# Attention and a mixture of experts on one core: score products in two row halves over three banks, a second norm one step later, fewer small vector operations

## The chip, the cores and the metric

One core of one Trainium2 chip. The metric is the device time of one execution, in microseconds. The programs are written directly against the engines: TensorE (PE), VectorE (DVE), ScalarE (ACT), GpSimd (POOL) and SyncE (SP) each have their own list of instructions, and semaphores hold them together.

## What is computed

`x` and `ctx` are 32 batches of 64 tokens with 128 features, float32. First comes cross attention with 16 heads of 8 features, then a mixture of 16 experts with two chosen per token plus one shared expert, each on a layer norm and each added to `x`:

```python
qh, kh, vh = heads(layernorm(x) @ Wq.T), heads(ctx @ Wk.T), heads(ctx @ Wv.T)
scores = einsum('bhqd,bhkd->bhqk', qh, kh) / scale          # scale = 8 ** -0.5
scores = where(mask, -1e9, scores)
x = x + merge(softmax(scores) @ vh) @ Wo.T
flat = layernorm(x)
top, idx = top_k(flat @ router_w.T + router_bias, 2)
combine = scatter(softmax(top), idx)                         # tokens x 16 experts
out = sum_k combine[:, k] * ((silu(flat @ gate_k) * (flat @ up_k)) @ down_k)
x = x + out + (silu(flat @ sh_gate.T) * (flat @ sh_up.T)) @ sh_down.T
```

## The kernel before, in words

The 2048 tokens are 16 tiles of 128 rows, two batches each. Everything that feeds a float32 product of the experts is split into a high and a low part (`w_hi`, `w_lo`, `xt2_hi`, `xt2_lo`, `hid_hi`, `hid_lo`), so that three fast products stand for one exact one.

**Projections.** Four groups of four tiles: first norm on DVE (`norm1`, `scale1`, L634 to L651), transposes, masks, and the products for V, Q and K on TensorE (`project`, L872). Q and K land in `q_all` and `k_all` with the features of eight heads in 64 rows for one batch and 64 for the other, and two halves of the heads one behind the other.

**Attention, the pipeline of 16 steps.** Each engine has a function `step(t, p, on)`; `on(lag)` says whether tile `t - lag` exists. In step `t`:

- POOL masks Q and K of tile `t + 2` into `q_blk` and `k_blk` (`q_block`, `k_blocks`, L414 to L430), and finishes the second norm's factors of tile `t - 2`.
- PE (L936 to L1003) makes the two score products of tile `t + 1` (128 rows, 512 columns each, `scores(g)`, L964), transposes the two halves of the probabilities of tile `t` (`transposes(h)`, L945), multiplies them with V (`values(h)`, L954), turns the value sums of tile `t - 1` back into rows (`values_as_rows`, L914), transposes its attention row (`attention_transposed`, L919) and projects it (`output_projection`, L924), and for tile `t - 2` transposes the second norm (`norm_transposed`, L930) and makes the router product (`router`, L934).
- DVE (L700 to L771) adds the projection to `x` (L705), adds the router's bias (L708), takes the moments of the second norm (L713, L721) and the two best experts (L717 to L733), takes the row maxima of the scores (L738), subtracts them (L759), and divides the value sums (L747, L749).
- ACT (L532 to L574) copies the transposed probabilities (L542), scales the second norm (L554), copies the transposed attention row (L558) and the transposed second norm twice (L564, L565), takes the exponentials (L547), copies the value sums (L570), and casts a piece of the expert weights (L538).

**What sets the order.** The order of calls in these functions, written out by hand, engine by engine; each engine works through its list in order. PSUM has eight banks; two of them hold scores (`score_ps`), so that the first score product of the next tile may be written once DVE has subtracted that of this one.

**Experts.** Four groups of 512 tokens, nine units each (the shared expert and eight pairs): `gate`, `up`, `down` on PE (L1028 to L1073), SiLU and the high part on ACT (`silu`, `high_part`), product, low part and weight on DVE (`product`, `low_part`, `weighted`). The first units run between the last steps of the attention; this stretch, from step 15 to the first dense units, is called the hand-over below. Outside the pipeline's loop the last steps are called by `peel(step, TILES)` and so on.

## Time and profile before

| | |
|---|---|
| median of 3 runs | 193.76 us (193.52 to 194.12) |
| the profiled execution | 194.68 us, span 192.9 us |
| PE busy | 179.3 us (93% of the span) |
| DVE busy | 168.8 us (87%) |
| ACT busy | 124.6 us (65%) |
| POOL busy | 92.1 us (48%) |
| chain that ended last | PE 61%, DVE 19%, ACT 5%, issue 5% |

The span is what the profile sees of the profiled execution; the rest of its time lies around it. An engine's busy time is the union of its instructions. A product on TensorE in float32 appears as two records, a transpose as one; their ends are modelled, so it is the distance from one start to the next that tells what one costs. The stages: projections to about 34 us, attention to about 103, the hand-over to about 124, experts to the end.

### The profile page before, as it was taken

How to read it: one execution, taken by the hardware profiler on the slowest of the kernel's cores; microseconds unless marked ns; L12 is line 12 of the kernel's file. 1: busy time of each engine (PE TensorE's matmuls, PEld its weight loads, DVE VectorE, ACT ScalarE, POOL GpSimd, SP SyncE). 2: the span in 40 equal slices, each digit the busy share in tenths (PEclk: the TensorE clock that was granted, in tenths of full speed). 3: DMA queues.
4: the chain of work that ended last, by engine and by line, in shares of the span. 5: the costliest groups of instructions: out<-in, count | busy, mean ns of one | idle time of the engine just before them, and what ended most of it. 6: DMA issues, size and time to landing. Idle time of an engine off the chain costs nothing.

```text
span 192.9 us, 4173 instructions
## 1 busy us (share of the span) xinstructions
PE 179.3 (93%) x1351; PEld 131.8 (68%) x1351; DVE 168.8 (87%) x515; ACT 124.6 (65%) x280; POOL 92.1 (48%) x148
## 2 busy tenths in 40 slices
PE   7599599999999999999998799999999999999962
PEld 7497467566666666666666466778888888888841
DVE  6899999589999999989995799988899889988981
ACT  2168374777888888888885855466655665565641
POOL 5746992758988988888786690300000000000000
PEclk9969979999999999999999999999999999999997
DMA  5984910000000000000000174332363236324401
GB/s 135 286 249 92 352 40 0 5 0 0 3 2 5 0 3 0 3 0 2 5 0 3 57 198 139 110 110 82 128 180 115 72 126 171 120 82 126 120 0 54
DMA packets 13202, 15.33 MB, mean 79 GB/s; under 512 B 1665, under 2 KB 8193, under 8 KB 13057
## 3 DMA queue, kind: packets, MB, share of 16 engines
q1 hardware_dynamic: 12608, 14.57, 24.8%
q10 hardware_dynamic: 576, 0.55, 1.2%
q8 instruction: 9, 0.15, 0.3%
q14 instruction: 9, 0.07, 0.1%
HBM read 13.93 MB, written 1.18 MB: 78 GB/s over the span
## 4 chain that ended last, share of the span: by engine, by line
PE 61%; DVE 19%; ACT 5%; issue 5%; POOL 0%; DVEq 0%; POOLq 0%
PE bank L1013 26%; PE bank L964 12%; PE bank L945 5%; PE bank L954 5%; DVE hid L823 2%; PE bank L903 2%; ACT hid_hi L598 2%; PE bank L934 2%; DVE prob L759 2%; PE bank L924 2%; DVE smax L738 2%; DVE xn L649 2%; DVE hid_lo L815 2%; DVE cmix_sb L823 2%; PE bank L893 1%
## 5 line engine op out<-in xcount | busy, mean ns | idle before, releaser
L589 ACT ACTIVATE sig<-bank 128x512 f32<-128x512 f32 x36 | 21.5, 600 | 21.0 <-PE bank L1013 20.4
L964 PE MATMUL bank<-k_blk,q_blk 128*128 128x512 f32 x64 | 34.0, 615 | 0.0
L426 POOL TENSOR_TENSOR k_blk<-k_all,consts_sb 128x512 f32<-128x512 f32 x32 | 32.7, 1045 | 0.0
L1013 PE MATMUL bank<-xt_hi,w_hi 128*128 (+1 forms) x72 | 29.1, 405 | 0.0
L1013 PE MATMUL bank<-xt_lo,w_hi 128*128 (+1 forms) x72 | 28.4, 394 | 0.0
L1013 PE MATMUL bank<-xt_hi,w_lo 128*128 (+1 forms) x72 | 28.3, 393 | 0.0
L542 ACT COPY prob_t<-bank 128x512 f32<-128x512 f32 x32 | 18.8, 586 | 11.5 <-PE bank L945 11.5
L806 DVE TENSOR_TENSOR hid_u<-sig,bank 128x512 f32<-128x512 f32 x32 | 21.9, 684 | 4.2 <-PE bank L1013 2.5
L738 DVE TENSOR_REDUCE smax<-bank 128x8 f32<-128x512 f32 x32 | 21.9, 686 | 2.6 <-PE bank L964 2.6
L759 DVE TENSOR_TENSOR prob<-bank,smax 128x512 f32<-128x512 f32 x32 | 22.0, 687 | 0.6
L547 ACT ACTIVATE prob<-prob 128x512 f32<-128x512 f32 x32 | 20.8, 653 | 0.0
L945 PE MATMUL bank<-consts_sb,prob 128*128 128x128 f32 x128 | 19.2, 273 | 0.0
L598 ACT CAST hid_hi<-hid 128x512 fp32r<-128x512 f32 x24 | 14.9, 621 | 6.4 <-DVE hid L823 6.4
L815 DVE TENSOR_TENSOR hid_lo<-hid,hid_hi 128x512 fp32r<-128x512 f32 x24 | 16.7, 697 | 1.7 <-ACT hid_hi L598 1.0
L1013 PE MATMUL bank<-hid_hi,w_hi 128*128 128x512 f32 (+1 forms) x37 | 15.1, 409 | 2.2 <-DVE hid_lo L815 2.2
L945 PEld LDWEIGHTS bank<-consts_sb,prob 128*128 128x128 f32 x128 | 15.1, 141 | 1.1 <-issue 1.1
L1013 PEld LDWEIGHTS bank<-xt_hi,w_lo 128*128 128x128 f32 x72 | 13.5, 188 | 3.0
L1013 PEld LDWEIGHTS bank<-xt_hi,w_hi 128*128 128x128 f32 x72 | 13.6, 189 | 2.8
L1013 PEld LDWEIGHTS bank<-xt_lo,w_hi 128*128 128x128 f32 x72 | 13.6, 188 | 2.7
L1013 PE MATMUL bank<-hid_hi,w_lo 128*128 128x512 f32 (+1 forms) x37 | 14.4, 390 | 0.0
L1013 PE MATMUL bank<-hid_lo,w_hi 128*128 128x512 f32 (+1 forms) x37 | 14.4, 388 | 0.0
L823 DVE TENSOR_TENSOR hid<-hid_u,mix_all 128x512 f32<-128x512 f32 x20 | 13.9, 697 | 0.0
(116 smaller groups left out, 378.8 us busy)
## 6 DMA issues: line engine op xcount, KB each, us to landing
mix_all<-w_rows SPq DMA_DIRECT2D x64, 128.0 KB, 2.9
w_moe_sb<-w_moe SPq DMA_DIRECT2D x1, 1728.0 KB, 9.9
x_sb<-x SPq DMA_DIRECT2D x4, 256.0 KB, 7.6
ctxt_sb<-ctx_t SPq DMA_DIRECT2D x4, 256.0 KB, 5.9
ctx_sb<-ctx_nat SPq DMA_DIRECT2D x4, 256.0 KB, 5.1
out<-x_sb SPq DMA_DIRECT2D x3, 256.0 KB, 2.3
w_att_sb<-w_att ACTq DMA_DIRECT2D x1, 264.0 KB, 5.8
mrow<-mask_row ACTq DMA_DIRECT2D x1, 256.0 KB, 4.9
```

The lines of the kernel that those rows point to most:

```text
L426: last = nc.gpsimd.tensor_tensor(k_blk[p][:, g, :, :], k_all[:, bass.ds(t, 1), g, :].broadcast_to([P, HG, S]), hmask_sb.rearrange("p (h o) ...
L542: nc.scalar.copy(prob_t[p][:, h * GT:(h + 1) * GT, :], pt_ps[h][:, :].rearrange("p (j q) -> p j q", q=P)).then_inc(s_pt_sb[h], 1)
L547: nc.scalar.activation(prob[q][:, g * GN:(g + 1) * GN], prob[q][:, g * GN:(g + 1) * GN], ACT.Exp, scale=SCORE_SCALE).then_inc(s_exp[g], 1)
L589: nc.scalar.activation(sig[r][:, :], gate_ps[r][:, :], ACT.Silu).then_inc(s_sig, 1)
L738: nc.vector.tensor_reduce(smax[q][:, g * HG:(g + 1) * HG], score_ps[g][:, :].rearrange("p (h s) -> p h s", s=S), AX_X, ALU.max).then_inc(s ...
L759: nc.vector.tensor_tensor(prob[q][:, g * GN:(g + 1) * GN].rearrange("p (h s) -> p h s", s=S), score_ps[g][:, :].rearrange("p (h s) -> p h ...
L806: nc.vector.tensor_tensor(dst[:, :], sig[r][:, :], up_ps[r][:, :], ALU.mult).then_inc(s_hid_u, 1)
L815: nc.vector.tensor_tensor(hid_lo[k][:, cols], hid[k][:, cols], hid_hi[k][:, cols].bitcast(F32), ALU.subtract).then_inc(s_hid_lo, 1)
L823: nc.vector.tensor_tensor(hid[m % 3][:, :], hid_u[r][:, :], spread[k], ALU.mult).then_inc(s_hid, 1)
L945: last = nc.tensor.transpose(pt_ps[h][:, j * P:(j + 1) * P], prob[p][:, c:c + P], ident_sb)
L964: nc.tensor.matmul(score_ps[g][:, :], q_blk[q][:, g, :, :].rearrange("p b s -> p (b s)"), k_blk[q][:, g, :, :].rearrange("p h s -> p (h s) ...
L1013: last = nc.tensor.matmul(out, w, moving, start=start and k == 0, stop=stop and k == 2)
```

## The change

- **Scores.** Q and K are laid out so that the heads of half `g` stand in rows `64 g` to `64 g + 63`, 32 rows for each batch and four heads, with the other four heads behind them in the columns. A score product has 64 rows and 256 columns; four of them make what two made, `g = 0` in the upper row half and `g = 1` in the lower, each into a bank of its own. Three banks take turns. All four stand at the head of the step, before the transposes.
- **K mask** on POOL: one operation with four heads instead of two with eight. The Q and K projections become eight products of 32 output rows instead of four of 64.
- **Second norm.** Its transpose, its two copies, the router and the low part move from tile `t - 2` to tile `t - 3`, the choice of experts to `t - 4`; there is one more step at the end (`TRAIL` 4).
- **Small operations.** The router's bias is added by a second product (a row of ones with a row of biases) into the same sum, so that DVE reads the logits in PSUM. The negated mean goes into POOL's operation. `gap` and `top_f` are made for four tiles at a time.
- **Order.** On ACT the copies of the second norm come before the second half's, and the scaling of the norm last. On DVE the attention row comes before the first row maximum. The transfer of the bias goes.

```diff
-        score_ps = banks[5:7]
+        score_ps = [banks[5], banks[6], banks[3]]
+
+        def score_bank(tile, g):
+            return score_ps[(2 * tile + g) % 3]
...
-        at_ps, wo_ps, tail_ps = (bank[:, 0:P] for bank in banks[2:5])
+        at_ps, wo_ps, tail_ps = banks[2][:, 0:P], banks[2][:, P:2 * P], banks[4][:, 0:P]
...
+        logit_ps = banks[4][:, P:P + EXPERTS]
...
             def k_blocks(t, p):
 
-                for g in range(2):
-                    last = nc.gpsimd.tensor_tensor(
-                        k_blk[p][:, g, :, :],
...
+                nc.gpsimd.tensor_tensor(
+                    k_blk[p][:, :, :, :],
...
-                    nc.gpsimd.tensor_tensor(bias2[p][:, :], neg_mean2[p][:, :], rstd2[p][:, :], ALU.mult).then_inc(s_bias2, 1)
+                    nc.gpsimd.tensor_scalar(bias2[p][:, :], mv2[p][:, 0:1], rstd2[p][:, :], -1.0, ALU.mult,
+                                            ALU.mult).then_inc(s_bias2, 1)
...
-                if on(3):
-                    dve.wait_ge(s_logit, t - 2)
-                    nc.vector.tensor_tensor(logit[q][:, :], tail_ps[:, 0:EXPERTS], bias_sb[:, :],
-                                            ALU.add).then_inc(s_logit_sb, 1)
+                if on(4):
+                    dve.wait_ge(s_logit, t - 3)
+                    nc.vector.max(top_v[:, t - 4, :], logit_ps).then_inc(s_top_v, 1)
...
+                if on(4) and (t - 3) % GT == 0:
+                    tiles = slice(t - 3 - GT, t - 3)
+                    nc.vector.tensor_tensor(gap[:, tiles], top_v[:, tiles, 1], top_v[:, tiles, 0], ALU.subtract)
+                    dve.wait_ge(s_top_i, t - 3)
+                    nc.vector.tensor_copy(top_f[:, tiles, :], top_i[:, tiles, 0:2]).then_inc(s_top_f, 1)
...
-            dve.wait_ge(s_wproj, 32)
...
             def attention_transposed(t, p):
                 pe.wait_ge(s_att, t + 1)
+                if t > 0:
+                    pe.wait_ge(s_x1, t)
...
-                    pe.wait_ge(s_logit_sb, t)
+                    pe.wait_ge(s_top_i, t)
                 nc.tensor.transpose(tail_ps, xn2[p][:, :], ident_sb).then_inc(s_xt2, 1)
 
             def router(t, p):
                 pe.wait_ge(s_xt2_hi, t + 1)
-                nc.tensor.matmul(tail_ps[:, 0:EXPERTS], xt2[p][:, :], wr_sb, start=True, stop=True).then_inc(s_logit, 1)
+                nc.tensor.matmul(logit_ps, ones_sb[:, :], bias_row_sb, start=True, stop=False)
+                nc.tensor.matmul(logit_ps, xt2[p][:, :], wr_sb, start=False, stop=True).then_inc(s_logit, 1)
...
+                def scores():
+
+                    for j in range(2):
+                        for g in range(2):
+                            freed = 2 * (t + 1) + g - 3
+                            if j == 0 and freed >= 0:
+                                pe.wait_ge(s_sub[freed % 2], freed // 2 + 1)
+                            rows = slice(g * ROWS, (g + 1) * ROWS)
+                            last = nc.tensor.matmul(score_bank(t + 1, g)[:, j * HQ * S:(j + 1) * HQ * S],
+                                                    q_blk[q][rows, j, :, :].rearrange("p b s -> p (b s)"),
+                                                    k_blk[q][rows, j, :, :].rearrange("p h s -> p (h s)"),
+                                                    start=True, stop=True, tile_position=(g * ROWS, 0))
+                            if j == 1:
+                                last.then_inc(s_score[g], 1)
...
                     pe.wait_ge(s_blk, t + 2)
-                    scores(0)
+                    if t == 0:
+                        pe.wait_ge(s_q_sb, GROUPS)
+                    scores()
```

**TensorE, one step in the middle of the attention.** `prob` are the probabilities that are transposed, `pvt_sb` the value sums, `xn_0` or `xn_1` the second norm, `ones_sb` the row for the bias. Before:

```order
L945 MATMUL bank<-consts_sb,prob 128x128 x4
L964 MATMUL bank<-k_blk,q_blk 128x512
L919 MATMUL bank<-consts_sb,att 128x128
L945 MATMUL bank<-consts_sb,prob 128x128 x4
L930 MATMUL bank<-consts_sb,xn_1 128x128
L924 MATMUL bank<-w_att_sb,att_t 128x128
L954 MATMUL bank<-prob_t,v_all 18x64 x16
L934 MATMUL bank<-w_att_sb,xt_1 128x16
L964 MATMUL bank<-k_blk,q_blk 128x512
L914 MATMUL bank<-consts_sb,pvt_sb 128x128 x2
```

And in the change:

```order
L934 MATMUL bank<-consts_sb,prob 128x128 x4
L900 MATMUL bank<-consts_sb,pvt_sb 128x128 x2
L918 MATMUL bank<-consts_sb,xn_0 128x128
L934 MATMUL bank<-consts_sb,prob 128x128 x4
L907 MATMUL bank<-consts_sb,att 128x128
L922 MATMUL bank<-w_att_sb,ones_sb 128x16
L923 MATMUL bank<-w_att_sb,xt_0 128x16
L912 MATMUL bank<-w_att_sb,att_t 128x128
L943 MATMUL bank<-prob_t,v_all 18x64 x16
L957 MATMUL bank<-k_blk,q_blk 128x256 x4
```

The second score product has left the place between the two halves' transposes, the router has moved ahead of the output projection, and the scores follow the value products directly.

**ScalarE, from the first half's copy to the exponentials of the next tile.** `xt` is the transposed second norm, `att_t` the transposed attention row. Before:

```order
L542 COPY prob_t<-bank 128x512
L554 ACTIVATE xn_0<-x_sb,bias_0,rstd_0 128x128
L558 COPY att_t<-bank 128x128
L542 COPY prob_t<-bank 128x512
L564 COPY xt_0<-bank 128x128
L565 CAST xt_hi<-bank 128x128
L547 ACTIVATE prob<-prob 128x512
```

And in the change:

```order
L543 COPY prob_t<-bank 128x512
L556 COPY xt_0<-bank 128x128
L557 CAST xt_hi<-bank 128x128
L543 COPY prob_t<-bank 128x512
L562 COPY att_t<-bank 128x128
L565 ACTIVATE xn_1<-x_sb,bias_1,rstd_1 128x128
L548 ACTIVATE prob<-prob 128x512
```

The attention row's copy now stands behind both halves' copies and the two of the second norm; the norm itself stands behind it.

**TensorE in the hand-over**, from the second norm of tile 14 (`xn_0`) to the first down product (the rows that read `hid_hi` and `hid_lo`). In the change:

```order
L918 MATMUL bank<-consts_sb,xn_0 128x128
L1009 MATMUL bank<-xt_hi,w_hi 128x512
L1009 MATMUL bank<-xt_lo,w_hi 128x512
L1009 MATMUL bank<-xt_hi,w_lo 128x512
L922 MATMUL bank<-w_att_sb,ones_sb 128x16
L923 MATMUL bank<-w_att_sb,xt_0 128x16
L1009 MATMUL bank<-hid_hi,w_hi 128x512
L1009 MATMUL bank<-hid_lo,w_hi 128x512
L1009 MATMUL bank<-hid_hi,w_lo 128x512
```

Before, the router of tile 14 stood ahead of both the gate and the up products of the third unit; it now stands between the up products and the first down product.

## Rows read from the trace of the kernel before

**Rows 1.** Windows, attention stage: per engine busy us (records), granted clock, DMA share, GB/s.

```profile
60.00:75.00 15.00, 15.00 (x165) 10.05 (x165) 14.17 (x75) 12.29 (x34) 13.29 (x25) 1.00 0.01 2
```

**Rows 2.** Timeline of TensorE, one step; columns: start us, us, engine, line, operation.

```profile
60.93 0.60 PE L945 MATMUL bank<-consts_sb,prob 128*128 128x128 f32 x4
61.37 1.02 PE L964 MATMUL bank<-k_blk,q_blk 128*128 128x512 f32 x2
...
62.88 0.46 PE L924 MATMUL bank<-w_att_sb,att_t 128*128 128x128 f32 x2
63.27 0.78 PE L954 MATMUL bank<-prob_t,v_all 128*18 128x64 f32 x32
63.98 0.40 PE L934 MATMUL bank<-w_att_sb,xt 128*128 128x16 f32 x2
64.23 1.10 PE L964 MATMUL bank<-k_blk,q_blk 128*128 128x512 f32 x2
65.17 0.38 PE L914 MATMUL bank<-consts_sb,pvt_sb 128*128 128x128 f32 x2
65.39 0.60 PE L945 MATMUL bank<-consts_sb,prob 128*128 128x128 f32 x4
```

**Rows 3.** Timeline of ScalarE in the same step.

```profile
61.57 0.59 ACT L542 COPY prob_t<-bank 128x512 f32<-128x512 f32 x1 [0.55 <-PE bank L945]
62.05 0.50 ACT L554 ACTIVATE xn<-x_sb,bias,rstd 128x128 f32<-128x128 f32 x1
62.54 0.27 ACT L558 COPY att_t<-bank 128x128 f32<-128x128 f32 x1
62.97 0.59 ACT L542 COPY prob_t<-bank 128x512 f32<-128x512 f32 x1 [0.17 <-PE bank L945]
63.46 0.27 ACT L564 COPY xt<-bank 128x128 f32<-128x128 f32 x1
63.61 0.28 ACT L565 CAST xt_hi<-bank 128x128 fp32r<-128x128 f32 x1
```

**Rows 4.** Timeline of VectorE in step 13, where it does not wait.

```profile
91.35 0.28 DVE L705 TENSOR_TENSOR x_sb<-x_sb,bank 128x128 f32<-128x128 f32 x1
91.55 0.16 DVE L708 TENSOR_TENSOR logit<-bank,bias_sb 128x16 f32<-128x16 f32 x1
91.67 0.29 DVE L713 BATCH_NORM_STATS2 stats<-x_sb 128x6 f32<-128x128 f32 x1
...
92.27 0.14 DVE L727 TENSOR_TENSOR gap<-top_v 128x1 f32<-128x1 f32 x1
...
92.46 0.69 DVE L738 TENSOR_REDUCE smax<-bank 128x8 f32<-128x512 f32 x1
...
95.47 0.51 DVE L696 TENSOR_SCALAR w_top<-half_tanh 128x8 f32<-128x8 f32 x2
```

**Rows 5.** Timeline of TensorE, last K projection and the score product behind it.

```profile
32.81 1.03 PE L903 MATMUL bank<-cmix_sb,w_att_sb 128*64 128x256 f32 x8
33.77 1.13 PE L964 MATMUL bank<-k_blk,q_blk 128*128 128x512 f32 x2
```

**Rows 6.** The start: timeline of TensorE, and the chain that ended last.

```profile
9.34 1.90 PE L879 MATMUL bank<-w_att_sb,ctxt_sb 128*128 128x128 f32 x8 [2.19 <-DMA bias_sb<-router_bias]
...
19.14 3.61 DVE xn L649 x4
```

**Rows 7.** Hand-over to the experts: timelines of ScalarE and TensorE, and the chain.

```profile
103.68 0.49 ACT L554 ACTIVATE xn<-x_sb,bias,rstd 128x128 f32<-128x128 f32 x1 [1.18 <-POOL bias L469]
...
112.08 0.48 PE L1013 MATMUL bank<-hid_hi,w_hi 128*128 128x512 f32 x1 [0.26 <-DVE hid_lo L815]
...
112.64 0.62 ACT L598 CAST hid_hi<-hid 128x512 fp32r<-128x512 f32 x1 [0.87 <-DVE hid L823]
...
124.26 0.50 PE L1013 MATMUL bank<-hid_hi,w_hi 128*128 128x512 f32 x1 [0.18 <-DVE hid_lo L815]
...
134.34 18.80 PE bank L1013 x81
```

More of the change, by code:

```diff
@@ L623, in _ @@
             slot(0, 3)
+            peel(step, TILES + 2)
             slot(0, 4)
@@ L958, in values @@
                     return last
[L960 to L966 removed]
+                def scores():
+                    for j in range(2):
+                        for g in range(2):
[9 more added lines that the diff above has]
+                                last.then_inc(s_score[g], 1)
                 if on(-1):
                     pe.wait_ge(s_blk, t + 2)
[L970 removed]
+                    if t == 0:
+                        pe.wait_ge(s_q_sb, GROUPS)
+                    scores()
                 else:
@@ L973, in step @@
                     gate(0, 0)
+                if on(0):
+                    transposes(0)
                 if on(1):
```

197 lines of the change are left out of this document (84 added, 113 removed).

## The prediction

> **What bounds the kernel now.** I first read the windows of the attention stage: in the 15 us from 60 to 75, TensorE (PE) is busy 15.00, VectorE (DVE) 14.17, ScalarE (ACT) 12.29, GpSimd (POOL) 13.29, at a granted clock of 1.00, which is 2.4 GHz [rows 1]. That says "TensorE", but not why: a queue can be full because it is the bound, or because something in it is late and the rest is spread by waits of no length. So next comes the timeline of one step on TensorE [rows 2] and on ScalarE [rows 3]; I write T0 for the transposes of the first half of the probabilities, S0 and S1 for the two score products, WO for the output projection, V for the value products, R for the router, VR for the transposes of the value sums.
>
> One step is 65.39 - 60.93 = 4.46 us, from T0 to T0. On TensorE alone it is a closed row of starts: T0 0.44, S1 and what follows up to WO 1.51 (61.37 to 62.88), WO 0.39, V 0.71, R 0.25, S0 0.94, VR 0.22 [rows 2]. The same 4.46 also closes over ScalarE: T0 to its copy 0.64 (61.57), copy to second norm 0.48 (62.05), norm to copy of the attention row 0.49 (62.54), from there to WO 0.34 (62.88), then WO, V, R, S0, VR as above: 0.64 + 0.48 + 0.49 + 0.34 + 0.39 + 0.71 + 0.25 + 0.94 + 0.22 = 4.46 [rows 2, 3]. Two loops tie: the stretch from T0 to WO takes 1.95 either way. Shortening TensorE's own work there alone gives nothing, because WO also waits for ScalarE, and V and the next scores stand behind WO.
>
> DVE is a third pacer close behind. In step 13, where it doesn't wait, it needs 95.47 - 91.35 = 4.12 [rows 4].
>
> **The change, part by part.**
>
> *Score products.* Before: S0 takes 0.94 and S1 0.86, the 0.08 being a weight load that nothing hides; 1.80 a step [rows 2]. After: four products of 64 rows and 256 columns, two at a time in the two row halves. If nothing overlaps they stream as many columns as now: 2 x 0.86 + 0.08 + 0.10 for leaving the split shape = 1.90. If pairs overlap with no cost, 0.86. No row shows row halves; the nearest rows are the projections, whose two column halves are split in the same way: eight passes of 256 columns, which one after the other would take the 2 x 0.86 that the same number of columns takes in S1, go in 33.77 - 32.81 = 0.96 [rows 5]. So pairs overlap fully there, and 0.10 is lost on leaving the split. I take 0.96 + 0.08 for the load = 1.04, since this is the same engine and the same kind of split.
>
> *The new loop.* All scores now stand at the head of the step, straight after V; R and VR leave the path between V and T0, and ScalarE's order from T0 becomes copy, two router copies, copy, attention row, second norm. T0 to copy 0.64; copy 0.48; the two router copies 0.15 each (63.46 to 63.61), 0.30; second copy 0.49 (62.97 to 63.46); attention row to WO 0.34; WO 0.39; V 0.71; scores 1.04; together 4.39 [rows 2, 3]. T0 now follows a change of shape and loses the hiding of its first weight load, a few hundredths: I take 4.42. So 0.76 us of score time leave TensorE and the step falls by 0.04: T0 to WO grows from 1.95 to 2.28, and WO to T0 falls from 2.51 to 2.14. TensorE will stand idle before WO. With the bounds of the scores the step is 4.24 to 5.28. There are some 11 such steps (2 to 12): **-0.4 us**.
>
> *The small VectorE operations.* The bias add goes (0.12, 91.55 to 91.67), gap, negated mean and index copy go out of the step (0.19, 92.27 to 92.46) and come back as two wider ones every fourth step; one pause goes; but the row maximum now stands straight before the subtraction that reads it, 0.1 more than with another operation between. 4.12 becomes about 3.95 [rows 4]. In the steps that go at 4.42 this is idle time and gives nothing; where DVE also carries the expert weights (steps 12 to 14) it gives 0.1 to 0.2 a step: **-0.4 us**. The bias moves to a second small product on TensorE, some 0.2 by R's 0.25, in the idle time before WO: nothing; if WO were not late it would cost 0.2 a step.
>
> *Added waits.* The transpose of the second norm now waits for DVE's index search of the tile before; behind it stand the second half's transposes and so the loop. The search ends some 0.75 after DVE's step begins (now 92.27 - 91.35 = 0.92, less the bias add and a pause) [rows 4], the transpose stands 0.66 behind T0 (0.44 + 0.22), and TensorE's step begins before DVE's: nothing, at the worst a tenth. The attention row's transpose also waits for the residual sum of the tile before, which DVE does ahead of that attention row: nothing. The first scores wait once for the last copy of Q, priced under the start.
>
> *The masked keys* on GpSimd are one operation instead of two. It is busy 13.29 of 15 and nobody on the loop waits for it [rows 1]: nothing. Neither is there a cost if that cover goes, for the work shrinks.
>
> *The start.* The bias transfer, for which TensorE waited 2.19 us before its first projection, is gone. The chain there runs over VectorE's first norm (3.61 us of it at 19.14), which waits for none of this [rows 6]: nothing. DVE's attention row now stands before the maximum and waits for VR behind the scores; the first steps lose what they won on S: nothing, between -0.4 and +0.4.
>
> *The hand-over to the experts.* Two effects. ScalarE's copy of the attention row 14 no longer stands behind a norm that waited 1.18 for GpSimd [rows 7]; about half of that, 0.6, reaches the expert weights and the first SiLU. Against that, R of tile 14 now stands ahead of the first down product, and its copies stand on ScalarE behind the high part of the next hidden tile. That cast starts at 112.64, when the weighted tile is there, and takes 0.62; the two copies 0.15 + 0.28, the way to TensorE 0.07 (62.81 to 62.88), R with its bias 0.45: the down product at 114.2 instead of 112.08, less the 0.8 from the steps and the 0.6 from above: 112.8 [rows 2, 3, 7]. From the first down product to the sixth there are five units of nine products; before, with stalls, 124.26 - 112.08 = 12.2. By the dense stretch (81 in 18.80, so 2.09 a unit) they need 10.5, with the norms and routers that remain 11.2: 124.0 [rows 7]. The experts, dense from there on, start their steady stretch 0.2 earlier than now, though the attention ends 0.8 earlier: the hand-over costs **+0.6 us**, bounds -0.6 (nothing but the norm's wait counts) and +1.6 (each of the three late routers holds TensorE 0.35 longer).
>
> *Sum.* -0.4 - 0.4 + 0.6 = -0.2 on the profiled execution's 194.68 us. That one is 0.92 over the median 193.76 of the three runs shown, so the forecast is **193.6 us**: no change that can be told. A measurement of this kernel tells about 0.3% (0.6 us) from none.
>
> **A rule weighed.** The projections overlap wholly [rows 5]. The Trainium skill (TensorE: Matmul & The Clock Gate, Part 3) tells of four row tiles that gained 3.07 times, not four, that is 77% of the ideal. If row halves here behave so, the estimate for the pairs is 0.86 / 0.77 = 1.12, with load and exit 1.30, and the step 4.68: the forecast by that rule is 196.4. The row decides for the point; the rule's case is a rival below, worked out without it as well.
>
> **The rivals.**
> 1. *The pairs cost little more than their columns* (faster). Scores near 0.86 to 0.95, the step near 4.24: 11 x 0.22 = 2.4, so -2.4 - 0.4 + 0.6: 191.6. For it: the 0.96 includes an exit that row halves may not pay. Against it: S0's unhidden load. 0.20.
> 2. *TensorE's own sum was the bound, not the loop* (faster). Then the step falls to DVE's 3.95: 11 x 0.5 = 5.5, so -5.5 - 0.4 + 0.6: 188.5. For it: TensorE is full [rows 1]. Against it: WO still waits for the attention row in ScalarE's new order, 2.25 after T0, which no shorter product changes. 0.10.
> 3. *The pairs overlap only in part* (slower). Every 0.1 us that the scores take over 1.08 makes the step longer than 4.46, since WO, V, scores and T0 follow one another. If each of the four pairs shows its weight load, they take 0.96 + 4 x 0.08 = 1.28 and the step 4.66: 11 x 0.20 - 0.4 + 0.6 = +2.4: 196.2. For it: each half loads 128 columns, the projections' halves 64, and a step has three changes of shape, not two. Against it: the projections show no such loss [rows 5]. 0.13.
> 4. *They do not overlap at all*, which would be the change not doing what it says: scores 1.90, step 5.28, 11 x 0.82 + 0.2 = +9.2: 203.0. Against it: [rows 5]. 0.06.
> 5. *The hand-over costs its upper bound*, +1.6, because the three late routers each hold TensorE: -0.8 + 1.6: 194.6. 0.10.
>
> My own forecast, with scores between 0.98 and 1.10, lies between 193.0 and 194.4: 0.41, of which 0.32 are within 0.3%, 0.05 faster, 0.04 slower.
>
> **How the numbers follow.** Faster: 0.20 + 0.10 + 0.05 = 0.35. Slower: 0.13 + 0.06 + 0.10 + 0.04 = 0.33. The same: 0.32. The range 190.6 to 196.8 holds rivals 1, 3 and 5 and the forecast; it leaves out rivals 2 and 4, together 0.16, and some edges. The likeliest case alone is 193.0 to 194.4.
>
> **What would show it.** Right: in the profile after, steps of about 4.42; TensorE idle some 0.3 before WO, ended by the copy of the attention row; VectorE idle about 0.45 a step, ended by VR; the scores about 1.04 from first start to T0, their passes starting in pairs; an idle TensorE before R of tile 14 in the hand-over, and the sixth down product near 124. Wrong: steps at or under 4.2 with VectorE full mean that the loop is not there; scores of 1.3 or more mean that the halves do not run together; a sixth down product away from the end of the attention by another distance than today means that the hand-over was mis-sized.

## The result: slower by 1.5%, just past the end of the range

The kernel after the change took 196.84 us (median of 4 runs, 196.62 to 197.35), the kernel before, in 4 runs, 193.82 (193.52 to 194.12): a ratio of 1.0146, 95% interval 1.0105 to 1.0187. The forecast was 193.6 in 190.6 to 196.8. Here and below, ratios and intervals are worked out from the single runs, without those of a slower state, and need not be the quotient of the two medians. The profiled execution of after took 197.35 with a span of 195.5; before it was 194.68 and 192.9, so the spans differ by 2.6.

The page of after, its span, its busy times and the granted clock in 40 slices:

```profile
span 195.5 us, 4400 instructions
...
PE 174.4 (89%) x1511; PEld 135.5 (69%) x1511; DVE 164.5 (84%) x443; ACT 125.5 (64%) x280; POOL 76.3 (39%) x132
...
PEclk9999879999999999999999978999999999999998
```

TensorE is busy for 4.9 us less than before (179.3) and the program is longer. The clock has a dent at the 24th and 25th slice, where attention hands over to the experts. (The dents at the 5th and 6th slice and at the end lie outside the stretch that is compared below.)

TensorE's timeline of one attention step of after:

```profile
63.44 1.13 PE L957 MATMUL bank<-k_blk,q_blk 64*128 64x256 f32 x8
64.50 0.66 PE L934 MATMUL bank<-consts_sb,prob 128*128 128x128 f32 x4
64.99 0.38 PE L900 MATMUL bank<-consts_sb,pvt_sb 128*128 128x128 f32 x2
...
65.32 0.60 PE L934 MATMUL bank<-consts_sb,prob 128*128 128x128 f32 x4
66.05 0.33 PE L907 MATMUL bank<-consts_sb,att 128*128 128x128 f32 x1
...
66.42 0.38 PE L923 MATMUL bank<-w_att_sb,xt 128*128 128x16 f32 x2
66.83 0.49 PE L912 MATMUL bank<-w_att_sb,att_t 128*128 128x128 f32 x2
67.25 0.67 PE L943 MATMUL bank<-prob_t,v_all 128*18 128x64 f32 x32
67.85 1.13 PE L957 MATMUL bank<-k_blk,q_blk 64*128 64x256 f32 x8
```

The step is 67.85 - 63.44 = 4.41, where [rows 2] had 4.46; the four score products take 64.50 - 63.44 = 1.06. The step came as forecast. The loss must lie behind the loop, so next I read the hand-over: when the last subtraction of attention starts on VectorE, and from there to the sixth down product on TensorE. VectorE's end of attention in after:

```profile
99.05 0.69 DVE L745 TENSOR_TENSOR prob<-bank,smax 128x512 f32<-128x512 f32 x1
99.65 0.69 DVE L322 TENSOR_TENSOR comb<-comb,w_top 128x128 f32<-128x128 f32 x1
...
101.66 0.17 DVE L718 FIND_INDEX8 top_i<-top_v,bank 128x8 uint32<-128x16 f32 x1
...
102.25 0.29 DVE L734 TENSOR_TENSOR att<-bank,inv_den 128x128 f32<-128x128 f32 x1
```

And TensorE from there on, with the idle time before an instruction and what ended it in brackets:

```profile
101.98 0.30 PE L918 MATMUL bank<-consts_sb,xn 128*128 128x128 f32 x1 [1.42 <-DVE top_i L718]
...
103.25 0.27 PE L907 MATMUL bank<-consts_sb,att 128*128 128x128 f32 x1
...
105.27 0.33 PE L1022 MATMUL bank<-consts_sb,comb 128*128 128x128 f32 x1
...
108.75 0.40 PE L922 MATMUL bank<-w_att_sb,ones_sb 128*128 128x16 f32 x2 [1.24 <-ACT xt_hi L557]
...
113.52 0.40 PE L922 MATMUL bank<-w_att_sb,ones_sb 128*128 128x16 f32 x2 [1.86 <-ACT xt_hi L557]
...
113.99 0.48 PE L1009 MATMUL bank<-hid_hi,w_hi 128*128 128x512 f32 x1
...
116.07 0.45 PE L918 MATMUL bank<-consts_sb,xn 128*128 128x128 f32 x1 [0.23 <-DVE top_i L718]
...
117.60 0.63 PE L1009 MATMUL bank<-hid_hi,w_hi 128*128 128x512 f32 x1
118.03 0.63 PE L1009 MATMUL bank<-hid_lo,w_hi 128*128 128x512 f32 x1
118.46 0.49 PE L1009 MATMUL bank<-hid_hi,w_lo 128*128 128x512 f32 x1
...
126.87 0.50 PE L1009 MATMUL bank<-hid_hi,w_hi 128*128 128x512 f32 x1
```

The kernel before in the same places, the last subtraction and the attention row on VectorE:

```profile
99.40 0.69 DVE L759 TENSOR_TENSOR prob<-bank,smax 128x512 f32<-128x512 f32 x1
...
103.03 0.29 DVE L749 TENSOR_TENSOR att<-bank,inv_den 128x128 f32<-128x128 f32 x1
```

and on TensorE the transposes of that row, of the expert weights (`comb`) and of the last second norm:

```profile
103.38 0.33 PE L919 MATMUL bank<-consts_sb,att 128*128 128x128 f32 x1 [0.80 <-DVE att L749]
...
105.64 0.31 PE L1025 MATMUL bank<-consts_sb,comb 128*128 128x128 f32 x1
...
113.72 0.33 PE L930 MATMUL bank<-consts_sb,xn 128*128 128x128 f32 x1
```

The last subtraction starts 0.35 earlier than before. The first down product starts at 113.99 instead of 112.08, the sixth at 126.87 instead of 124.26 [rows 7]. From the last subtraction to the sixth down product it is 27.8 instead of 24.9: the hand-over lost 3.0, and -0.35 + 3.0 is the whole difference of the spans. Two things are new. The second norm's transpose of tile 12, early in step 15, waits 1.42 for VectorE's index search, which stands behind the expert weights; and products near 117 to 118 start 0.43 apart where the dense stretch has 0.23. The windows of after on TensorE (busy, granted clock, DMA share, GB/s):

```profile
108.00:112.00 4.00, 2.64 (x13) 1.00 0.37 119
112.00:116.00 4.00, 2.32 (x10) 0.91 0.64 198
116.00:120.00 4.00, 3.93 (x15) 0.67 0.24 76
120.00:124.00 4.00, 4.00 (x19) 1.00 0.21 70
```

From 112 to 116 the engine worked 2.32 of 4 (3.92 before), then a part of the products ran at 1.2 GHz; before, the clock was 1.00 in all four windows. So the theory I went into the experiments with had three shares: the wait of the norm's transpose for the search behind the expert weights; the router of tile 14 ahead of the first down product, which I had forecast; and the half clock.

### The profile page after: what moved, and what is told of

The parts are those of the page before. It is cut to its first block, busy times and chain, and to the rows that moved or that the text cites. A ratio compares the mean times of both kernels' runs of the same rounds, so it can differ in the third digit from the quotient of the medians.

```text
span 195.5 us, 4400 instructions
## 1 busy us (share of the span) xinstructions
PE 174.4 (89%) x1511; PEld 135.5 (69%) x1511; DVE 164.5 (84%) x443; ACT 125.5 (64%) x280; POOL 76.3 (39%) x132
## 4 chain that ended last, share of the span: by engine, by line
PE 64%; DVE 13%; ACT 6%; issue 4%; DMA 3%; DVEq 0%; SPq 0%
PE bank L1009 31%; PE bank L957 9%; PE bank L934 5%; PE bank L943 5%; PE bank L912 3%; DVE xn L651 2%; ACT hid_hi L599 2%; DVE hid L807 2%; DVE att L734 2%; PE bank L907 2%; PE bank L900 2%; DVE inv_den L732 2%; ACT prob_t L543 2%; DVE cmix_sb L807 1%; DMA mix_all<-w_rows 1%
## 5 line engine op out<-in xcount | busy, mean ns | idle before, releaser
L590 ACT ACTIVATE sig<-bank 128x512 f32<-128x512 f32 x36 | 21.4, 598 | 27.1 <-PE bank L1009 26.8
L1009 PE MATMUL bank<-xt_hi,w_hi 128*128 (+1 forms) x72 | 29.7, 413 | 0.0
L548 ACT ACTIVATE prob<-prob 128x512 f32<-128x512 f32 x32 | 20.1, 631 | 7.3 <-DVE prob L745 7.1
L934 PE MATMUL bank<-consts_sb,prob 128*128 128x128 f32 x128 | 19.9, 279 | 0.0
L957 PE MATMUL bank<-k_blk,q_blk 64*128 64x256 f32 x128 | 18.1, 402 | 0.4 <-ACT q_all L526 0.4
L599 ACT CAST hid_hi<-hid 128x512 fp32r<-128x512 f32 x24 | 14.9, 621 | 5.2 <-DVE hid L807 5.1
L934 PEld LDWEIGHTS bank<-consts_sb,prob 128*128 128x128 f32 x128 | 14.3, 141 | 5.2 <-issue 5.0
L428 POOL TENSOR_TENSOR k_blk<-k_all,consts_sb 128x512 f32<-128x512 f32 x16 | 16.6, 1040 | 0.0
```

The source lines that it names most:

```text
L548: nc.scalar.activation(prob[q][:, g * GN:(g + 1) * GN], prob[q][:, g * GN:(g + 1) * GN], ACT.Exp, scale=SCORE_SCALE).then_inc(s_exp[g], 1)
L590: nc.scalar.activation(sig[r][:, :], gate_ps[r][:, :], ACT.Silu).then_inc(s_sig, 1)
L599: nc.scalar.copy(hid_hi[k][:, cols], hid[k][:, cols]).then_inc(s_hid_hi, 1)
L934: last = nc.tensor.transpose(pt_ps[h][:, j * P:(j + 1) * P], prob[p][:, c:c + P], ident_sb)
L957: last = nc.tensor.matmul(score_bank(t + 1, g)[:, j * HQ * S:(j + 1) * HQ * S], q_blk[q][rows, j, :, :].rearrange("p b s -> p (b s)"), k_b ...
L1009: last = nc.tensor.matmul(out, w, moving, start=start and k == 0, stop=stop and k == 2)
```

## The experiments

All are edits of the kernel after. "The stretch" is the time from the start of the last subtraction to the start of the sixth down product, each from the profiled run: 24.9 before, 27.8 in the change. Times are medians, ratios are to the kernel before on the same chip, where its median lay between 193.97 and 194.64.

**The change once more.** No edit.

> The change itself once more, beside the kernels of this call. If the half clock belongs to the order of the hand-over, the profile again shows products 0.43 apart near 115 to 119 and the total is 1.010 to 1.019 times the kernel before. If it was chance, clock 1.00 there and about 1.2 us less: 1.004 to 1.010.

197.48, ratio 1.0131 (1.0068 to 1.0195). The windows of its profiled run (columns as in [rows 1]):

```profile
112.00:116.00 4.00, 2.75 (x9) 2.36 (x10) 3.52 (x8) 1.34 (x4) 3.58 (x4) 0.60 0.62 187
116.00:120.00 4.00, 4.00 (x15) 3.12 (x13) 1.37 (x3) 1.44 (x4) 0.46 (x1) 0.55 0.19 66
```

The half clock is there again, and longer (0.60 and 0.55): the stretch is 29.1. Its four runs took 195.78, 196.74, 198.23 and 198.26 at mean clocks of 0.991, 0.978, 0.970 and 0.970. So the half clock belongs to this hand-over, but its length differs from run to run. That it also carries the spread of the four runs is likely and not shown: the mean clock is that of the whole span, with its dents at the start and the end, and only one run of a kernel is profiled.

**The router of tile 14 moved.**

```diff
             up(0, 2)
-            router(TILES - 2, 0)
             pe.wait_ge(s_ct_sb, 1)
             down(0, 2)
+            router(TILES - 2, 0)
             gate(0, 3)
```

> The whole loss (+2.6 us of span) came after the attention loop: the first down product started at 113.99 instead of 112.08 and the sixth at 126.87 instead of 124.26. Here the router product of tile 14 goes behind the first down product on TensorE instead of ahead of it. Theory A (three shares: the early norm transpose behind the expert weights, the router of tile 14 ahead of the first down product, and a half clock that follows): the wait of 1.86 before the router is only shortened by the 0.7 of down work that now lies in it, so the first down product starts near 111.7 (no wait of the router), the sixth 0.7 earlier than in the change, and up to 1.6 more if the half clock goes with the wait: total 194.5 to 196.1. Rival B (this router alone made the loss): all of 2.6 comes back, 194.2. Rival C (the half clock alone made it, waits do not matter): 196.8, nothing moves.

197.52, ratio 1.0175 (1.0132 to 1.0217): nothing gained. The first down product came at 111.13, the sixth at 126.68, the stretch is 28.0. Counted from the last subtraction, which started 0.39 earlier in this run (98.66), the first down product came 2.5 earlier than in the change. In its timeline of TensorE the wait is in two places now, the second being the last norm's transpose behind this router (0.23 in the change):

```profile
113.27 0.40 PE L922 MATMUL bank<-w_att_sb,ones_sb 128*128 128x16 f32 x2 [1.27 <-ACT xt_hi L557]
...
115.81 0.45 PE L918 MATMUL bank<-consts_sb,xn 128*128 128x128 f32 x1 [1.13 <-DVE top_i L718]
```

Rival B falls, and so does the share of 0.7 that theory A gave this router.

**The expert weights behind the attention row on VectorE.**

```diff
-                if isinstance(t, int) and t == TILES - 2:
+                if isinstance(t, int) and t == TILES - 1:
                     dve.wait_ge(s_w_top, 1)
                     weigh_experts(nc.vector, 0)
                     join_experts(dve, nc.vector, 0)
```

> In step 15 VectorE does its work on the expert weights (1.40 us, 99.65 to 101.05 in the change) after the attention tile instead of ahead of the router search, so TensorE's norm transpose of tile 12 no longer waits for that search behind the weights. Theory A: the wait of 1.42 before that transpose goes; the output projection of tile 14, the transpose of the expert weights (105.27 in the change) and the DMA chain behind it all come 1.4 earlier, first down product near 112.6, total 1.4 lower than the change (195.4) and up to 1.6 lower again if TensorE's clock then stays at full (193.8). Rival B (the router of tile 14 made the loss): the router still waits, total 196.8 to 196.5. Rival C (half clock alone): 196.8 unless the clock changes.

196.13, ratio 1.0086 (1.0051 to 1.0120). The wait of 1.42 is gone and the first down product stands at 112.70, as expected; but the clock was 0.50 from 112 to 116 and 0.67 after, and the stretch stayed at 27.8. The single edits mix the waits with the clock, so the clock had to be held.

**Both edits.**

> Both edits of the hand-over together: the expert weights after the attention tile in VectorE's step 15, and the router of tile 14 behind the first down product on TensorE. Theory A: the shares add, 1.4 and 0.7, and the half clock (8 products 0.43 apart instead of 0.23, 1.6 us) probably goes: 193.2 to 194.7, near the kernel before. The first down product near 110.5 and the sixth at 123.2 to 124.8. Rival (the steps or the start made the loss): stays above 196.

194.32, ratio 0.9999 (0.9967 to 1.0032). Here the runs lie in two groups, 193.7 to 195.3 and 196.1 to 196.9; the profiled one, at 196.88, is of the upper group, has the half clock (0.79 and 0.78 from 112 to 120), and its stretch is 27.1.

**Dummy products in the waits.** Products of ones by ones into a free bank, whose results nobody reads, 5 ahead of the router of tile 13, 8 ahead of that of tile 14.

```diff
+            def stay_warm(products):
+                for _ in range(products):
+                    nc.tensor.matmul(banks[1][:, 0:P], ones_sb[:, :], ones_sb[:, :], start=True, stop=True)
```

> Only the clock is touched: 5 products of ones in a free bank ahead of the router of tile 13 and 8 ahead of that of tile 14, in the 1.24 and 1.86 us in which TensorE waits for the high part of the transposed tile; nothing else moves. If the granted clock of 0.67 from 116 to 120 is a cost of its own that follows from the idle stretches before it, the clock stays at 1.00, the sixth down product comes up to 1.6 earlier and the total is 195.2 to 196.0. If the waits alone make the loss and VectorE or ScalarE would be late anyway, the clock may stay at 1.00 and the total remains at 196.8. If the clock falls for another cause, neither changes.

195.59, ratio 1.0076 (1.0044 to 1.0108). The clock is 1.00 in every window from 100 to 128, and the stretch is 26.7, 1.1 less, though what the waits wait for is as late as before. Its two ends, on VectorE and on TensorE:

```profile
98.44 0.69 DVE L745 TENSOR_TENSOR prob<-bank,smax 128x512 f32<-128x512 f32 x1
```

```profile
125.13 0.50 PE L1013 MATMUL bank<-hid_hi,w_hi 128*128 128x512 f32 x1
```

The half clock is a cost of its own. The same shows without an edit to the hand-over in a run described below, in which the clock happened to stay up.

**The two edits apart, clock held.** The router's edit with 5, 4 and 4 dummy products (ahead of both routers and of the last norm's transpose), and the weights' edit with 5 and 8. The places in the router's:

```diff
+            stay_warm(5)
             router(TILES - 3, 1)
...
             down(0, 2)
+            stay_warm(4)
+            router(TILES - 2, 0)
             gate(0, 3)
+            stay_warm(4)
             norm_transposed(TILES - 1, 1)
```

> The router of tile 14 behind the first down product, with dummy products in the waits ahead of the routers of tiles 13 and 14 and of the last norm transpose. With dummies alone it took 26.69 from the start of the last subtraction to the sixth down product, with both edits 25.30. If this router is the larger share: 25.4 to 25.9. If the wait only moves to the norm transpose of tile 15 (in the run of this edit without dummies that wait grew from 0.23 to 1.13): 26.4 to 27.0, total as with dummies alone, 195.0 to 196.0.

> The expert weights after the attention tile on VectorE, with the dummy products. If the early wait (1.42) is a share of its own: 25.2 to 25.6 from the last subtraction to the sixth down product, total 193.8 to 194.8, as good as both edits together. If the transfer of the expert weights hides it: 26.3 or more.

The router's edit: 195.57, ratio 1.0050 (1.0025 to 1.0075), stretch 26.7, just as with dummies alone. The weights' edit: 194.10, ratio 0.9984 (0.9959 to 1.0008), stretch 25.4. Its two ends, and the transpose of the expert weights:

```profile
98.93 0.69 DVE L745 TENSOR_TENSOR prob<-bank,smax 128x512 f32<-128x512 f32 x1
```

```profile
103.75 0.33 PE L1026 MATMUL bank<-consts_sb,comb 128*128 128x128 f32 x1
...
124.32 0.50 PE L1013 MATMUL bank<-hid_hi,w_hi 128*128 128x512 f32 x1
```

With the clock at 1.00 in both, the weights' edit, in which the early wait is gone, wins 26.7 - 25.4 = 1.3, and the router's place nothing. But 1.3 is not the price of that wait against the kernel before. From the last subtraction to the transpose of the expert weights it is 6.24 before (105.64 - 99.40), 6.22 in the change (105.27 - 99.05) and 4.82 with the edit (103.75 - 98.93): the edit also takes the weights from ahead of the attention row, where the kernel before has them too, and so comes out ahead of both.

**Both edits and dummies.** 5 and 10 dummy products.

> Both edits of the hand-over, and dummy products of ones on TensorE in the two waits that are left (5 ahead of the router of tile 13, 10 ahead of that of tile 14). With both edits alone the profiled run stood at a granted clock of 0.79 and 0.78 from 112 to 120, 6 products there started 0.43 apart, and its runs lay at either 193.7 to 194.6 or 196.1 to 196.9. Theory (the clock is a cost of its own, on top of the waits): with the clock at 1.00 throughout, the sixth down product starts near 124.2 and all runs lie together at 192.8 to 193.8. Rival (the two groups of runs have another cause): the runs stay apart, up to 196.9.

194.20, ratio 0.9987 (0.9965 to 1.0010); its ten runs lie between 193.82 and 194.96, without an upper group, and the stretch is 25.3. The sixth down product is at 123.77, 0.4 earlier than expected, and yet the total is 0.4 above the range given: the kernel before stood at 194.64 here, 0.8 above its median on the first chip.

**What is left: the transfer of the expert weights.** In both runs VectorE has the expert weights behind the attention row, as above. First the router of tile 14 behind the fourth gate and up products; then also the weights' transpose ahead of the output projection of step 15, with its copy ahead of the norm's scaling, and the router of tile 14 behind the fourth gate product alone.

```diff
+            gate(0, 2)
             router(TILES - 3, 1)
             output_projection(TILES - 1, 1)
-            gate(0, 2)
-            norm_transposed(TILES - 2, 0)
             up(0, 2)
-            router(TILES - 2, 0)
+            norm_transposed(TILES - 2, 0)
...
             gate(0, 3)
-            norm_transposed(TILES - 1, 1)
             up(0, 3)
+            router(TILES - 2, 0)
             down(0, 3)
...
```

The second, on TensorE and on ScalarE (where tile 14 is also copied ahead of the high part of unit 2):

```diff
+                if once and t == TILES - 1:
+                    weights_as_rows(0)
                 if on(1):
                     output_projection(t - 1, q)
...
+                if isinstance(t, int) and t == TILES - 1:
+                    weights_to_sbuf(0)
                 if on(2):
                     act.wait_ge(s_bias2, t - 1)
...
```

> The hand-over alone, no dummy products: expert weights after the attention tile, and on TensorE the router of tile 14 behind the fourth gate and up products, the third gate product ahead of the router of tile 13, the norm transposes of tiles 14 and 15 one product later. From the start of the last subtraction to the sixth down product it took 24.86 before, 27.83 in the change (26.62 in a run of the same hand-over whose clock stayed at 1.00), 25.29 with both edits and dummies. Theory (what was left was the wait of 2.4 for the tile behind the transfer of the expert weights): 23.8 to 25.0, clock at 1.00, total 192.8 to 194.4. Rival (the wait only moves to the next product, or the clock falls): 26 or more, total 195 to 197.

> As the run before, and the expert weights are transposed and copied in step 15 ahead of the output projection and the second norm's activation (instead of behind the values), so their transfer starts 1.0 to 1.4 earlier; ScalarE copies tile 14 ahead of the weighted unit's high part. Theory (the transfer sets when VectorE can weigh the first unit and so when TensorE is filled): from the last subtraction to the sixth down product 22.8 to 24.2, total 191.8 to 193.6. Rival (VectorE's own work from then on sets it): no better than the run before.

The first: 193.77, ratio 0.9979 (0.9954 to 1.0004), clock 1.00 without a dummy, stretch 25.1, just past the expected end. The second: 192.74, ratio 0.9938 (0.9913 to 0.9963), stretch 23.8, 1.1 less than the kernel before needs. So what is left of the loss seems to hang on the moment at which the expert weights are sent: with their transfer earlier by the edit, VectorE's wait of 1.02 for it is gone and the stretch is shorter. That is the likeliest reading and not shown alone, since the second run moves ScalarE's copy and the router of tile 14 as well.

**The score products in another order.** The two of one row half, then the two of the other.

```diff
-                    for j in range(2):
-                        for g in range(2):
+                    for g in range(2):
+                        for j in range(2):
```

> The four score products of a tile in another order: both of the first row half, then both of the second, so that only neighbours at the turn can lie beside each other. In the change the block of 8 records took 1.06 as if the two row halves ran wholly beside each other. Theory (the overlap is of pairs that stand next to each other in the order): the block takes 1.6 to 1.9, the step grows by 0.5 to 0.8 from 4.41, attention ends 8 to 12 later: total 204 to 209. Rival (TensorE reorders or queues per row half, so that order does not matter): block 1.06, total 196.8. Rival (the step has slack on TensorE): block longer, total less than 2 higher.

196.99, ratio 1.0169 (1.0103 to 1.0235): as the change. The block on TensorE, and the transposes behind it:

```profile
63.12 1.14 PE L957 MATMUL bank<-k_blk,q_blk 64*128 64x256 f32 x8
64.19 0.66 PE L934 MATMUL bank<-consts_sb,prob 128*128 128x128 f32 x4
```

64.19 - 63.12 = 1.07. The order in which the program names the halves does not matter; single records start in pairs, one of each row half: 6 ns apart in the change, 13 ns here. By chance this run kept its clock: its hand-over is that of the change, with waits of 1.41, 1.85 and 0.44 where the change had 1.42, 1.86 and 0.23, and TensorE's windows read

```profile
112.00:116.00 4.00, 2.33 (x12) 1.00 0.59 194
116.00:120.00 4.00, 4.00 (x21) 1.00 0.18 68
```

Its stretch is 26.6. Against the change's 27.8 that prices the half clock at 1.2, as the dummy products do.

**What sets the step.** Four runs, because the first two fell against me. First the rows ahead of the first transposes:

```diff
-                if on(0):
-                    transposes(0)
                 if on(1):
...
                     values_as_rows(t - 1)
+                if on(0):
+                    transposes(0)
```

> Inside the loop only: TensorE turns the values of the tile before into rows ahead of the first probability transposes instead of behind them. In the change VectorE waits 0.26 a step for these rows (they start at 64.99, it is free at 65.15) though their input was ready at 63.97. Theory (the steady step is not set by TensorE's own sum but by the round scores, transposes, rows, reciprocal, attention tile, output projection): the step falls by that wait from 4.41 to 4.15 to 4.20 and attention ends 2.9 to 3.6 earlier, total 193.2 to 194.2. Rival (TensorE's sum bounds the step, as the forecast took it): its own work is unchanged, the step stays at 4.35 or more and the total above 196.

198.01, ratio 1.0169 (1.0115 to 1.0222), a step of 4.62. Longer, so the theory behind it was wrong. TensorE's timeline shows the new wait, and the copies of the tile on ScalarE that end it come behind the first transposes:

```profile
60.60 0.60 PE L934 MATMUL bank<-consts_sb,prob 128*128 128x128 f32 x4
...
62.22 0.40 PE L922 MATMUL bank<-w_att_sb,ones_sb 128*128 128x16 f32 x2 [0.36 <-ACT xt_hi L557]
```

With the hand-over's edits and dummies the step is the same 4.62, and the stretch 25.8:

> The rows ahead of the transposes in the loop, both edits of the hand-over, and the dummy products. If the shares add: 193.2 to 194.2 for the loop, 3.0 to 4.0 less for the hand-over with the clock at full: 189.2 to 191.2, below both kernels. If the loop's gain is given back in the hand-over (the transfer of the expert weights sets the first down product, not the end of attention): 192 to 193.5.

196.97, ratio 1.0132 (1.0096 to 1.0168). Then the other round alone: half of the value products into TensorE's idle time, and the attention row's copy earlier on ScalarE.

```diff
-                if on(3):
-                    router(t - 3, q)
-                if on(1):
-                    output_projection(t - 1, q)
...
                     values(0)
+                if on(3):
+                    router(t - 3, q)
+                if on(1):
+                    output_projection(t - 1, q)
+                if on(0):
                     values(1).then_inc(s_pvt, 1)
...
-                if on(0):
-                    transposed(1)
                 if on(1):
                     act.wait_ge(s_at, t)
...
+                if on(0):
+                    transposed(1)
```

> The loop alone. Turning the values into rows first made the step 4.62, not 4.15: TensorE then waited 0.36 for the high part of the transposed tile, because the first probability transposes, their copy on ScalarE and the tile's copies behind it all came 0.27 later. So theory now: the step is the round scores, first transposes, ScalarE's copies (probabilities, tile, high part), router, output projection, values, with a second round through rows, reciprocal and the attention tile as long as it; TensorE idles 0.3 in both. Here the first half of the value products goes ahead of the router and the output projection into that idle time, and ScalarE copies the transposed attention tile ahead of the second half of the probabilities. Step 4.09 to 4.20, attention ends 3 to 4 earlier than in the change, total 192.8 to 194.0. Rival (TensorE's own sum sets the step): 4.41, total 196.8.

197.04, ratio 1.0150 (1.0082 to 1.0218), a step of 4.48: against me again. VectorE waits for the rows longer than in the change: 0.32 in the step shown, which also makes `gap` and `top_f` (0.26 in such a step of the change), and 0.45 in the others (0.39):

```profile
64.79 0.26 DVE L732 RECIPROCAL inv_den<-bank 128x16 f32<-128x16 f32 x1 [0.32 <-PE bank L900]
```

So two rounds of equal length tie, and both must be cut. Both together:

> The loop alone: rows ahead of the first transposes, and the first half of the value products ahead of the router with the transposed attention tile copied ahead of the second probabilities. Each alone lengthened the step (4.62 and 4.48 against 4.41): the first because the round through the first transposes, ScalarE's three copies, router, output projection and values grew by the rows' 0.27, the second because the round through rows, reciprocal and attention tile grew by the value products' change of tile form (0.14). Theory (two rounds of equal length; shortening one alone cannot gain): together 4.15 to 4.25, attention ends 2 to 3 earlier, total 193.5 to 195. Rival (TensorE's own sum, now with two more changes of tile form, sets it): 4.4 to 4.5, total 196.5 to 198.

> The loop of both_rounds with the last hand-over (weights sent earlier, router of tile 14 one product later). With the hand-over alone it took 192.74 (0.994 of the kernel before). Theory: 2 to 3 less, 189.5 to 191, 0.977 to 0.985 of the kernel before. Rival (the step does not fall): 192.5 to 193.5.

The loop alone: 193.72, ratio 0.9951 (0.9917 to 0.9986), 3.1 to 3.8 below the change's two medians. TensorE's scores of one step and the next, and the windows of the stage (columns as in [rows 1]):

```profile
61.56 1.14 PE L957 MATMUL bank<-k_blk,q_blk 64*128 64x256 f32 x8
...
65.78 1.13 PE L957 MATMUL bank<-k_blk,q_blk 64*128 64x256 f32 x8
```

```profile
60.00:75.00 15.00, 14.85 (x218) 11.68 (x220) 14.08 (x53) 13.26 (x38) 10.92 (x21) 1.00 0.01 2
```

The step is 65.78 - 61.56 = 4.22; every fourth takes 4.32, the mean is 4.25. VectorE's wait for the rows is gone in the step that makes `gap` and `top_f` and 0.19 or 0.28 in the others. The rival, TensorE's own sum at 4.41, falls. The hand-over of this run has the half clock (0.50 from 108 to 112, a stretch of 28.3), so the total shows the loop's gain in spite of it. With the last hand-over the gain reaches the end: **189.88, ratio 0.9770 (0.9729 to 0.9811), below both kernels**, as the first case expected it. The hand-over's last edits with the loop's second edit alone:

> The loop's edit and the last hand-over together: if the shares add, 3 to 4 less for the loop and 3.5 to 5 less for the hand-over than the change: 188.5 to 190.5, below both kernels. If the loop's gain is lost in the hand-over: 192 or more.

192.63, ratio 0.9934 (0.9905 to 0.9963): the second case, for the step was 4.48 there too. The page of the best version, both_rounds_and_handover:

```profile
span 188.4 us, 4400 instructions
...
PE 173.6 (92%) x1511; PEld 134.4 (71%) x1511; DVE 164.3 (87%) x443; ACT 123.6 (66%) x280; POOL 76.7 (41%) x132
...
PEclk9999979999999999999999999999999999999995
```

It does the change's work, and the dent in the clock between attention and experts is gone.

## Why the prediction was wrong, step by step

- **Score products: right.** 1.04 forecast, 1.06 measured; rivals 1, 3 and 4 fell. The estimate of 1.30 from the 3.07 of four in the Trainium skill (TensorE: Matmul & The Clock Gate, Part 3) was too high for this trace: by the 1.06, the two row halves in float32 overlap wholly.
- **The new loop: right in size, one name off.** 4.42 forecast, 4.41 measured. TensorE's idle time lies mostly ahead of the attention row's transpose (0.3), and only some 0.2 of it before the output projection (66.42 to 66.83 is 0.41, and 0.23 in the run of both rounds): a second round, over rows, reciprocal and attention row, is as long as the one I wrote down. VectorE waits 0.39 for the rows, and 0.26 in every fourth step, not 0.45. Rival 2, which had the step at VectorE's 3.95, fell with the 4.41; that TensorE's own sum does not set this step, the run of both rounds shows.
- **Small VectorE operations and start: right.** From the first residual sum (42.29; 41.86 before) to the last subtraction it is 0.78 less, forecast 0.8. In the profiled run the start gave 0.43 back, just over my upper bound of 0.4; with the same start it lay between 41.69 and 42.18 in other runs, so this is no settled cost.
- **Added waits: wrong, and this is the step that failed.** "The transpose of the second norm now waits for DVE's index search ... nothing, at the worst a tenth" was priced on a step of [rows 4] in which no expert weights stand ahead of the search. In step 15 they do (99.65 to 101.05), and TensorE's transposes, output projection, values and the transpose of the expert weights stand behind the wait. It measured 1.42 at the wait. Part of that reaches the path: from the start of attention row 14 on VectorE to its transpose on TensorE it is 1.00 (102.25 to 103.25), where it was 0.35 before (103.03 to 103.38). So the gain of 0.6 that I had forecast for the expert weights did not come: their transpose starts 6.22 after the last subtraction, 6.24 before. No run takes out this wait alone. The same added wait stands once more at the norm's transpose of tile 15, which starts 17.02 after the last subtraction (116.07) and 14.32 before (113.72); from there TensorE runs to the sixth down product without a wait. It waits for the search of tile 14, which stands behind a weighted unit on VectorE. This second place is read from the trace, not tested by itself. That VectorE carries the expert weights in steps 12 to 14 stood in my own text, one part further up.
- **Hand-over: right in kind, wrong in place and size.** I forecast +0.6 and named the router of tile 14. It does wait (1.86), and the first down product moved from 112.08 to 113.99. But that product is not what the end waits for: moved 2.5 earlier, it brought nothing at full clock (26.7 in both). The hand-over cost 1.8 at full clock (26.6 or 26.7 against 24.9), just over my bound of 1.6 and 1.2 more than forecast. Of these 1.2, 0.7 lie ahead of the first down product: I had it 14.2 after the last subtraction (112.8 less 98.6, which is 99.40 less the 0.8 of the steps), and it came after 14.9. That is about the gain of 0.6 that the added wait took. The other 0.5 lie behind it: 11.7 to the sixth down product at full clock, where I had 11.2.
- **The half clock: not in the prediction at all**, 1.2 of the 3.0 in the profiled run, 2.4 in that of the repeat. Rival 5 had the right place, but not this share. The Trainium skill (TensorE: Matmul & The Clock Gate, HAM oscillation) describes a kernel in which each wait for a transfer throws the engine back to half clock. The trace agrees in part: products stand 0.43 apart behind the wait of 1.86, but behind those of 1.42 and 1.24 in the same run the clock stayed at 1.00.

Summed: -0.35 to the end of attention, +1.8 for the hand-over at full clock, +1.2 of clock: +2.65, and the spans differ by 2.6. How the 1.8 divides between the added wait, the order of TensorE's queue and the transfer of the expert weights was not taken apart. The edit of VectorE's order wins 1.3 of it back; the last run of the hand-over alone wins back all of it and 1.1 more.

## What to carry to other kernels

A wait that costs nothing in the steady loop has to be priced again in each step that carries extra work on the engine waited for: walk the peeled steps one by one. Where a loop closes over two engines, look for the second round before cutting the first; here either cut alone made the step longer, and both together took 0.16 off the mean step. And when an edit adds idle time to TensorE, read the granted clock behind it, for the products after the wait can cost as much as the wait.

## What was not expected of the hardware

- The granted clock fell to 1.2 GHz behind single waits of 1.86 and 1.99 us in a stretch in which TensorE worked some 5 us of 8, and stayed at 2.4 GHz behind one of 1.85 in another run of the same hand-over. It also fell in a run whose longest wait there was 1.23 (rows_before_transposes, 0.50 from 112 to 116), so the length of one wait does not tell it. With dummy products in the waits it stayed up in five kernels of five, each profiled once.
- Products of the two row halves start side by side whatever their order in the program (1.06 and 1.07). The Trainium skill (TensorE: Matmul & The Clock Gate, Part 3, The mechanism) says that products start strictly in the program's order; the run with both products of one half first shows otherwise for products of different row halves.
- The same multiplication of the expert weights on VectorE took 0.69 at 99.65 in the change, while GpSimd worked on the low parts of the weights until 100.2, and 0.28 at 100.66 with both edits, behind that work:

```profile
100.66 0.28 DVE L322 TENSOR_TENSOR comb<-comb,w_top 128x128 f32<-128x128 f32 x1
```

The Trainium skill (SBUF — State Buffer, Who interferes with whom) says that the two engines share a pair of ports as an exclusive lock, and that a VectorE instruction with both inputs in SBUF contends with a GpSimd instruction that reads SBUF. The two rows agree with it, though no run here tried it alone.
